# First layer in one stage: its projections inside the steps of four heads, one pair of PSUM banks each for scores and transposed scores

## What is computed

```
xn = _layernorm(x)
x = x + _L0_attn_ref(xn, ...) + _L0_ffn_ref(xn, ...)
xn = _layernorm(x)
x = x + _L1_attn_ref(xn, ...) + _L1_ffn_ref(xn, ...)

# L0 attention (softmax over the keys k <= q)
scores = einsum('bhki,bhqi->bhkq', k, q) / sqrt(8); probs = softmax(where(mask, scores, -1e4), axis=2)
combined = einsum('bhkq,bhkl->bhql', probs, v);     out = combined @ out_w.T + out_b
# L0 ffn: both inputs of each product rounded in blocks of 32 that share an exponent
h = gelu(quant(x) @ quant(w_fc).T + b_fc); y = quant(h) @ quant(w_proj).T + b_proj   # 128 -> 512 -> 128
# L1: causal attention again; ffn is a sum over 8 experts of (silu(x@wg) * (x@wu)) @ wd
```

## Time and profile before

| | |
|---|---|
| median of 3 runs | 1597.89 us (1596.04 to 1610.23) |
| the profiled execution's own time | 1593.13 us, span of the core 1591.4 us |
| TensorE busy, all stages | 1425.7 us (90%), mean granted clock 0.927 |
| DVE, ACT, POOL busy | 1135.7 (71%), 787.5 (49%), 677.3 us (43%) |
| DMA | 97.55 MB, 61 GB/s in the mean |

### The profile page before, as it was taken

One profiled execution on the slowest core, in us unless ns is written; L12 is line 12 of the kernel. 1 busy time (PEld: TensorE's weight loads), 2 busy tenths in 40 slices (PEclk: granted clock), 3 DMA queues, 4 the chain that ended last, 5 costly groups with the idle time before them and its releaser, 6 DMA issues. The chain is left out here.

```text
span 1591.4 us, 23490 instructions
## 1 busy us (share of the span) xinstructions
PE 1425.7 (90%) x7944; PEld 818.4 (51%) x7944; DVE 1135.7 (71%) x3279; ACT 787.5 (49%) x1183; POOL 677.3 (43%) x784
## 2 busy tenths in 40 slices
PE   3788699999999956649999999999999999999987
PEld 1444344444444423426666666666666666666655
DVE  4887667767767726748787878777778787887843
ACT  2333245555555522216565656565655656565640
POOL 5555122222222213536455555455654554655540
PEclk9656589999999977869999999999999999999997
DMA  4322423333333212451112121111121211111003
GB/s 126 86 72 75 94 54 83 73 92 76 82 90 77 63 39 81 144 125 43 39 30 59 30 59 30 39 50 39 31 58 36 52 36 39 30 39 39 15 18 111
DMA packets 55333, 97.55 MB, mean 61 GB/s; under 512 B 8999, under 2 KB 19372, under 8 KB 52398
## 3 DMA queue, kind: packets, MB, share of 16 engines
q1 hardware_dynamic: 55214, 96.06, 23.7%
HBM read 51.98 MB, written 41.95 MB: 59 GB/s over the span
## 5 line engine op out<-in xcount | busy, mean ns | idle before, releaser
L206 POOL TENSOR_SCALAR_AFFINE_SELECT a_E<-a_E 128x256 f32<-128x256 f32 (+1 forms) x384 | 188.1, 493 | 555.0 <-ACT a_E L985 311.8
L1185 POOL TENSOR_TENSOR a_h_lo<-a_h,a_h_hi 128x512 fp32r<-128x512 f32 x256 | 329.3, 1286 | 150.2 <-ACT a_h_hi L1232 143.3
L182 DVE CUSTOM_DVE_ANT_0 bank<-bank,mask 128x512 f32<-128x512 f32 (+3 forms) x512 | 242.1, 516 | 117.6 <-PE bank L143 117.4
L1293 DVE SCALAR_TENSOR_TENSOR a_h<-a_h,bank 128x512 f32<-128x512 f32 x256 | 175.6, 686 | 150.9 <-ACT a_h L1228 150.9
L985 ACT ACTIVATE a_E<-bank_pair 128x1024 f32<-128x1024 f32 (+1 forms) x192 | 169.1, 881 | 173.4 <-PE bank_pair L153 173.2
L182 DVE CUSTOM_DVE_ANT_0 bank_pair<-bank_pair,mask 128x512 f32<-128x512 f32 (+3 forms) x512 | 238.0, 516 | 8.3 <-PE bank_pair L143 8.0
L1239 ACT ACTIVATE a_E<-bank_pair 128x1024 f32<-128x1024 f32 (+1 forms) x192 | 169.7, 884 | 134.3 <-PE bank_pair L153 134.1
L1369 PE MATMUL bank<-xT_hi,a_w_hi 128*128 128x512 f32 x512 | 215.3, 421 | 6.6 <-DVE a_h L1293 6.6
L1232 ACT ACTIVATE a_h_hi<-a_h 128x512 fp32r<-128x512 f32 x256 | 160.8, 628 | 118.3 <-DVE a_h L1299 116.6
L1371 PE MATMUL bank<-xT_lo,a_w_hi 128*128 128x512 f32 x512 | 203.7, 398 | 0.0
L1370 PE MATMUL bank<-xT_hi,a_w_lo 128*128 128x512 f32 x512 | 203.1, 397 | 0.0
(11 more groups left out here) (124 smaller groups left out, 1877.0 us busy)
## 6 DMA issues: line engine op xcount, KB each, us to landing
a_st<-stack_d SPq DMA_DIRECT2D x128, 160.0 KB
a_st<-stack_d SPq DMA_DIRECT2D x256, 64.0 KB
o_d<-a_O SPq DMA_DIRECT2D x64, 256.0 KB, 2.3
stack_d<-p_q_k_hi SPq DMA_DIRECT2D x48, 256.0 KB
stack_d<-p_q_k_lo SPq DMA_DIRECT2D x32, 256.0 KB
stack_d<-p_max_rows SPq DMA_DIRECT2D x2, 1024.0 KB, 9.3
a_st<-a_ms SPq DMA_DIRECT2D x128, 16.0 KB
at<-o_d SPq DMA_DIRECT2D x8, 256.0 KB, 3.6
```

Of the source, the lines that this page charges most:

```text
L182: ins = nc.vector.tensor_tensor_reduce(part, part, mask[:, N - w:N], 1.0, NEG, ALU.add, ALU.max, mx[:, g % 2, NT - 1 - kb, PLANES * r + j: ...
L206: return nc.gpsimd.affine_select(out=part, in_=part, compare_op=ALU.is_ge, fill=0.0, base=0, pattern=pattern, channel_multiplier=-1)
L1185: nc.gpsimd.tensor_tensor(h_lo[:, q % RH, :], h[:, q % RH, :], h_hi[:, q % RH, :].bitcast(F32), ALU.subtract).then_inc(h_lo_ready, 1)
L1293: nc.vector.scalar_tensor_tensor(hq, hq, 1.0, g_bank[:, :], ALU.add, ALU.mult).then_inc(silu_ready, 1)
```

## The change

`project(0)`, `attend` and `project(1)` become one block, `layer0`, that runs 46 steps, g from -7 to 38. Step g (b = g // 4, u = g % 4) holds the scores and maxima of quad g + 1, units 3 to 5 of T(g - 1), units 0 to 2 of T(g), and PV(g - 1). Between them stand one tile of the feed-forward part (q = g + 3), and by u the projections of three batches: of layer 0 for batch b + 2 or b + 1, of the attention's output for batch b - 1, of layer 1 for batch b - 2. `attend_moe` and `finish` stay as they are, but for the rows of the stacks; three of the stack buffers are now shared by both layers.

- The banks: `T_pair` (pair 0) holds every unit of T, `S_pair` (pair 1) every piece of scores and the transposed maxima, `W_pair` (pair 2) the projections and the first product of the feed-forward part, bank 6 PV, bank 7 the turned tiles and the second product. Before, T had two pairs and the scores three single banks.
- Scores are six pieces a quad, of both halves: `S(g, n)` waits until the maxima of piece n - 1 are taken. The causal mask is now added on PE, by one bf16 product of 128 columns for each block on the diagonal (8 pairs a quad), and DVE takes the maxima of a piece with one TENSOR_REDUCE of up to 1024 columns. Scores use 32 rows of a half and not 36.
- `T(g, n)` waits for the exp of the unit before it. The two bf16 products in front of each unit remain.
- The division of the attention's output takes the reciprocal sums through DRAM (`rden_d`) and a broadcasting load to `share`; POOL multiplies. The product L135 that spread them in layer 0 is gone.
- ACT makes the query and key parts straight from PSUM (two passes each) and the gelu of two tiles at a time; it changes its function table twice a batch.

```
-        def T_pair(g, n):
-            return pairs[(UNITS_A_QUAD * g + n) % 2]
+        T_pair, S_pair, W_pair, pv_bank, C_bank = *pairs, banks[6], banks[7]
+        A_bank, B_bank, M_bank = W_pair[:, 0, :], W_pair[:, 1, :], S_pair[:, 0, :]
...
-            def S(g, s):
-                j, n, r = s // 6, s // 2 % 3, s % 2
...
-                if S_place(g, s) >= 3:
-                    pe.wait_ge(*consumed(S_place(g, s) - 3))
-                scores(nc, S_bank(g, s), st, g % STACKS, n, r, j).then_inc(S_ready, 1)
+            def S(g, n):
+                if n == 0:
+                    pe.wait_ge(stack_in[g % STACKS], STACK_LOADS * (g // STACKS + 1))
...
+                    if g > 0:
+                        pe.wait_ge(mrow_ready, g)
+                else:
+                    pe.wait_ge(S_used, UNITS_A_QUAD * g + n)
+                t = NT - 1 - n % 2 if n < 4 else 5 - n
+                w = P * (t + 1)
+                for j in ((n // 2,) if n < 4 else range(PLANES)):
+                    at_col = j * N // PLANES if n >= 4 else 0
+                    for r in range(HALVES):
+                        rows = slice(HALF * r, HALF * r + SLOT_ROWS)
+                        nc.tensor.matmul(S_pair[:, r, at_col:at_col + w], st[g % STACKS][rows, j, 0, bass.ts(t, P)],
+                                         st[g % STACKS][rows, j, 1, 0:w], start=True, stop=False)
+                    for r in range(HALVES):
+                        ins = nc.tensor.matmul(S_pair[:, r, at_col + w - P:at_col + w], identb[:, :], mask[:, N - P:N], start=False, stop=True)
+                ins.then_inc(S_ready, 1)
...
             def T(g, n):
+                if g > 0 or n > 0:
+                    pe.wait_ge(exp_done, UNITS_A_QUAD * g + n)
...
                 if n == 0:
                     pe.wait_ge(mrow_in, MAX_LOADS * (g + 1))
-                if UNITS_A_QUAD * g + n >= 2:
-                    pe.wait_ge(exp_done, UNITS_A_QUAD * g + n - 1)
-                keep_warm(nc, T_pair(g, n), identb, mask)
-                keys_by_queries(nc, T_pair(g, n), st, g % STACKS, n % 3, n // 3).then_inc(T_ready, 1)
+                keep_warm(nc, T_pair, identb, mask)
+                keys_by_queries(nc, T_pair, st[g % STACKS], n % 3, n // 3).then_inc(T_ready, 1)
```

The step on DVE, in the new block (`magic_tile`, `unshift_tile` and `add_tile` are the tile's three parts):

```
+            for g, b, u in steps():
+                a, y1, y2, q = b + 2, b - 1, b - 2, tile_of(g)
+                S = in_range(g + 1)
+                if S:
+                    maxima_of(g + 1, 0)
+                if q is not None:
+                    magic_tile(q)
+                if S:
+                    maxima_of(g + 1, 1)
...
+                if S:
+                    maxima_of(g + 1, 3)
+                if q is not None:
+                    unshift_tile(WQ + q)
+                if S:
+                    maxima_of(g + 1, 4)
+                    maxima_of(g + 1, 5)
+                    negations(g + 1)
...
+                if q is not None:
+                    add_tile(q)
```

More of the change, by code:

```diff
@@ L61 @@
 VW = 32
-START = 2
 UNITS = [[(0, 0)], [(1, 128), (3, 0)], [(2, 0)]]
@@ L225, in build @@
         xT = sb("xT_hi", [P, B * N], F32R), sb("xT_lo", [P, B * N], F32R)
[L226 to L234 removed]
+        stacks = [sb(f"st{i}", [P, PLANES, 2, N], F32R) for i in range(MOE_STACKS)]
@@ L665, in _ @@
-            DVE_STEPS = 2 * NT + 2 * (1 + NT) if first else 2 * NT
-            def after():
-                if first:
-                    unshift_tile(B - 1, NT - 1)
-                    add_ffn(B - 1)
-            schedule(dve, before, batch, after)
+                    here.inc(nc.vector.bn_aggr(mv[layer][:, t, :], stats[layer][:, t, :]))
+                here.ready()
+                nc.vector.tensor_scalar(veps[layer][:, :], mv[layer][:, :, 1], LN_EPS, None, ALU.add).then_inc(var_ready[layer], 1)
@@ new lines, in _ @@
+                if u == 2:
+                    if ok(y2):
+                        values(y2)
+                    if ok(a):
+                        copy_xT(0, a)
+                if u == 1 and ok(y2):
+                    copy_xT(1, y2)
+                if in_range(g):
+                    exp(g, 0)
+                if q is not None:
+                    copy_tile(q)
+                if in_range(g):
+                    exp(g, 1)
+                    exp(g, 2)
+                if u == 1 and ok(y2):
+                    parts(1, y2, 0)
@@ L1116, in attend_moe @@
+def attend_moe(nc, xT, acc, experts, pairs, banks, consts, st, st_d, o_d):
     wg_in, wu_in, wd_in = experts
```

1321 lines of the change are left out of this document (620 added, 701 removed).

## The result

| | before | changed |
|---|---|---|
| median | 1600.28 us (1596.04 to 1610.23, 4 runs) | 1809.76 us (1803.23 to 1860.54, 4 runs) |
| profiled execution, span of the core | 1591.4 us | 1805.2 us |
| TensorE busy, mean granted clock | 1425.7 us, 0.927 | 1601.7 us, 0.845 |
| the stages of layer 0 | 688.0 us | 882.5 us |
| the experts' stage and `finish` | 903.4 us | 922.7 us |

The ratio is 1.1285, with an interval of 1.1208 to 1.1362: the changed kernel is 13% slower. The direction was forecast, the size was not: 1692 was forecast, with 1660 to 1755 as the range of its mechanism, and 1770 was the highest bound that it named.

A forecast was written before the change was run, and what follows sets the result against it. PE's own work was taken to bound `attend`, chains at a low clock the `project` stages. Ends of 140 us and 30 steps of 21.4 us (642) sum to 782 against 688, +94: 1692 us, range 1660 to 1755.

The forecast's parts named there:

- What bounds the kernel, and that waits are added: PE's own work bounds `attend`; in the merged stage waits for maxima and exps add 3.7 us a step.
- The chain of a step at full clock, 19.9 us: Merged stage: a bare step of 17.5 us plus projections of 4.1, 2.4, 0.9 and 2.0 us by u, mean 19.9.
- What half clock costs: Merged stage: a step bound by PE at half clock takes 1.61 times its 16.2 us of work, 26.1 us.
- the forecast's own formula: Mean step of the merged stage from both clocks: 1 / (0.7 / 19.9 + 0.3 / 26.1) = 21.4 us.
- How long the clock is low: Merged stage: half clock for three tenths of the time, mean clock between 0.75 and 0.95.
- Rival B: Merged stage: same chain, but waits of 1.2 us are too short to lower the clock; 1647 us, 23%.
- Rival C: Merged stage: waits are hidden and PE's work decides, 16.2 us a step; 1536 us, 24%.
- Rival D: Merged stage: the clock stays at half, 30 steps of 26.1 us; 1833 us, 11%.
- The table load at its own 1.28 us and no drain: ACT, ahead of the gelu: a load costs 1.28 us; the skill's drain would add an estimated 22 us.
- Four rows of the stacks: Experts' stage: score products with four rows fewer cost nothing, so the stage keeps its 903 us.
- The mask products: Merged stage: two bf16 products and a change of shape behind each of eight score pairs, about 0.2 us each.
- The ends: All outside steps 1 to 30 of the merged stage: 60 before step 0, 19, 13, 10 and 38; 140 us.

The follow-up runs named there:

- e4: The changed kernel with ten full-array bf16 products of 512 columns a step laid into waits of PE; 1731.25 us, ratio 1.078.
- e12: e4 with score products of 36 rows in both stages and six more added products in PE's wait for the gelu; 1671.47 us, ratio 1.040.
- e9: The changed kernel with each reduction of the maxima reading 128 columns of each half, most of the maximum left out; 1731.22 us, ratio 1.076.
- e16: The changed kernel with 36-row scores in both stages, maxima turned and copied earlier, PV spread over the step, no fillers; 1653.48 us, ratio 1.033.
- e6: The changed kernel with the gelu replaced by Identity, which needs no table load; 1792.60 us, ratio 1.108.
- e5: The kernel before, with 32 instead of 36 rows of the stacks in the experts' stage's score products; 1628.59 us, ratio 1.0152.
- e10: The changed kernel without the bf16 products that add the causal mask, 16 a step; 1745.85 us, ratio 1.085.
- e7: The changed kernel with scores waited for and reduced by halves, each mask product directly behind its score product; 1996.31 us, ratio 1.241.
- e18: The changed kernel with only the order changed: maxima turned and copied earlier, PV spread over the step; 1708.33 us, ratio 1.060.

## Why the forecast was right and wrong

- **What bounds the kernel, and that waits are added:** right. PE waits for the maxima and for their copy, 2.8 us a step with all other waits (some 3 were forecast), the reductions took what was assumed, and the first score product came at 48.7 us (not before 44).
- **The chain of a step at full clock, 19.9 us:** right. e4 (u = 0, 2 and 3) and e12 (u = 1) show 22.1, 20.9, 18.8 and 19.5 for u = 0 to 3 at clocks of 0.98 to 1.00, mean 20.3; forecast were 21.6, 19.9, 18.4 and 19.5. These steps hold fillers, laid into waits; no run shows the changed kernel's own chain at full clock throughout.
- **What half clock costs, 1.31 times that chain (26.1 to 19.9):** somewhat low. u = 1 took 27.6 us at a mean of 0.57 and 20.9 at 1.00 (e12). A mean of 0.57 is 87% of the time at half, so by the forecast's own formula a step at half throughout would take an estimated 29.0 us, 1.39 times.
- **How long the clock is low, "I take three tenths of the time":** this step failed. A mean clock of 0.71 is 59% of the time at half, and it lies below the 0.75 to 0.95 that the forecast gave as its sign. With it the formula of the forecast gives 1 / (0.41 / 19.9 + 0.59 / 26.1) = 23.1 us, 51 of the 82 us missing in the steps. With the chain of 20.3 and 1.39 times that at half, 28.2, it gives 24.3, and 24.1 was measured: the other 1.0 us a step are the price of half clock and the 0.4 by which the chain was longer, an estimate that rests on u = 1 alone. The choice rested on dense second halves that bring the clock back. Some did, but it fell again in the next first half, and behind the gelu it stayed at half for 23.9 us in which PE was busy for 23.0. At half clock the same products fill the time, so there a high busy share was no sign of a return.
- **Rival B, that waits of 1.2 us are too short to count:** shown wrong by the result and by e9, where shorter waits alone raised the clock. The Trainium skill ("TensorE: Matmul & The Clock Gate", Why this matters for your kernels) names only long idle gaps; here the longest wait of PE in steps 1 to 30 was 2.0 us, and the clock was at half for over half of the time. What would have come had the clock held is about e12, 1671 us, where rival B said 1647; e12 has 36 rows, though, which is worth some 18 us of the experts' stage, and fillers.
- **Rival C, PE's work decides:** wrong; in no run did a mean step come under the 18.3 us from which it wins, though u = 0 and u = 2 did in e16 (17.3 and 18.0).
- **Rival D, the clock stays at half, 1833 us:** the measured 1810 lies nearer to it than to the forecast, but its mechanism holds for 59% of the time only; at half throughout, 30 steps of an estimated 28.2 us would have taken 846 us and not 724.
- **The table load at its own 1.28 us and no drain:** right; in e16 the gelu starts 1.29 behind the load (474.16 and 475.45), and e6 gives 23 us for 13 loads, 1.8 each with whatever the clock adds.
- **"Four rows of the stacks, and I cost that at nothing, since the columns and the number of its products stay":** this failed too, by 20 us. Columns didn't tell the price of a product whose neighbours read another number of rows. The Trainium skill ("TensorEngine Tiling (Array Packing)", Key Properties) says that a change of tiling mode drains the engine; 32 and 36 rows fall into different ones. e5 agrees, with 22 us for 512 products, and so does the pair ahead of PV, where the rows change in either kernel and nothing was added. For the mask products I had charged a change of shape; here I had not.
- **The mask products, 1.6 us a step at full clock:** e10 shows 2.1 at a clock of 0.7, which fits: the step as a whole is 1.2 times its full-clock length there.
- **The ends:** 159 us against 140, with the clock at 0.50 in step 0 and 0.66 behind step 30.

None of the versions beats the kernel before (the lowest ratio is e16's 1.033). At full clock the ends (159) and 30 steps would have to stay under 688 us, 17.6 us a step; the best whole set had 19.6.

## What to carry to other kernels

Merging a thin stage into a dense one can cost the dense one its spare banks: with one pair for each kind of product, each round to the reader became a wait here, and with the granted clock falling behind them the low clock cost more (24.1 us a step against 20.3) than the waits themselves (2.8). Whether the merger would pay with the spare banks kept is not shown; no run had them. Don't guess the share of low clock from the busy share; look for the thinnest stretch of a period, allow for a clock that stays low behind it, and try the order of the work before adding products. When an operand loses a few rows, ask which tile of the array it now falls into, not only how many columns it streams.

## What the runs showed of the hardware

- Two score products on different row groups ran side by side as neighbours, 0.43 us for both, and one after the other with a 128-row product between them, 0.40 to 0.42 for each (e7).
- A pair of 32-row products of 512 columns ahead of a 36-row pair of 256 columns takes 0.65 us, a pair of 36-row ones 0.33; ahead of a 128-row product both take 0.43. Over 512 products it was 22 us (e5).
- Added products can shorten a kernel: ten of 512 columns a step, laid into waits, took 84 us off 30 steps (e4), and a better order without one product added took off 111 (e18).
